# Threshold arithmetic of a sparse-attention kernel: three steps per four heads moved from GpSimd to VectorE

## What is computed

```python
scores = einsum('bhqd,bhkd->bhqk', Q, K) / sqrt(16)       # 16 heads, 512 keys
thresh = top_k(scores, 31)[0][..., -1:]
scores = where(scores < thresh, -inf, scores)
context = einsum('bhqk,bhkd->bhqd', softmax(scores), V)
```

## Time and profile before

| what | value |
|---|---|
| median of three runs | 4140.59 us (4138.47 to 4140.77) |
| the profiled execution | 4140.48 us |
| its span, first to last instruction | 4138.7 us |
| granted TensorE clock, mean of the span | 0.977 |
| TensorE / VectorE / GpSimd / ScalarE busy | 94% / 93% / 86% / 85% of the span |
| the chain that ended last, by engine | PE 42%, POOL 31%, DVE 18%, ACT 4% |

### The profile page before, as it was taken

The page is one execution under the profiler, slowest core; times in us unless marked ns, Lnnn a source line. Parts: engine busy times, 40 slices in busy tenths (PEclk is TensorE's granted clock), DMA queues, the critical chain, the costliest instruction groups (busy, mean ns, idle before and its releaser), DMA issues.

```text
span 4138.7 us, 97302 instructions
## 1 busy us (share of the span) xinstructions
PE 3891.9 (94%) x31052; PEld 3201.5 (77%) x31052; DVE 3858.8 (93%) x15296; ACT 3530.2 (85%) x7749; POOL 3556.2 (86%) x4554
## 2 busy tenths in 40 slices
PE   6878999999999999999999999999999999998777
PEld 5656788888888888888888888888888888876566
DVE  3399999999999999999999999999999999999982
ACT  3389989989999998999999899999989999998872
POOL 1578999999999999999999999999999999987650
PEclk8889999999999999999999999999999999999988
DMA  3211221212222122222212222222222222121112
GB/s 108 54 34 35 56 63 53 63 56 62 54 58 63 52 63 55 62 55 58 63 52 63 55 60 58 57 61 54 61 56 60 57 58 60 54 50 28 31 29 57
DMA packets 243955, 230.71 MB, mean 56 GB/s; under 512 B 27123, under 2 KB 176628, under 8 KB 243316
## 3 DMA queue, kind: packets, MB, share of 16 engines
q1 hardware_dynamic: 243444, 224.49, 20.7%
HBM read 214.98 MB, written 9.44 MB: 54 GB/s over the span
## 4 chain that ended last, share of the span: by engine, by line
PE 42%; POOL 31%; DVE 18%; ACT 4%; issue 3%; DMA 1%; SPq 0%; POOLq 0%; ACTq 0%; DVEq 0%
PE pQ L592 15%; POOL HS L353 10%; POOL HL L965 5%; POOL HL L964 5%; PE pST L610 4%; PE pST L577 3%; POOL RB L364 3%; PE pFb L553 3%; PE pO L631 3%; DVE HL L915 2%; DVE HL L909 2%; DVE HL L905 2%; DVE HL L901 2%; DVE M L917 2%; DVE M L913 2%
## 5 line engine op out<-in xcount | busy, mean ns | idle before, releaser
L592 PE MATMUL pQ<-wf_sb,HS 128*128 128x192 f32 x8192 | 1474.9, 335 | 87.1 <-POOL HS L353 66.0
L592 PEld LDWEIGHTS pQ<-wf_sb,HS 128*128 128x128 f32 x8192 | 1361.6, 194 | 164.2 <-issue 107.2
L797 ACT ACTIVATE S<-S,edge 128x512 f32<-128x512 f32 x1024 | 743.3, 726 | 7.7 <-POOL edge L952 7.6
L803 ACT ACTIVATE S<-S,lift 128x512 f32<-128x512 f32 x1024 | 747.2, 730 | 1.9
L964 POOL TENSOR_TENSOR HL<-S,HL 128x512 f32<-128x512 f32 x512 | 657.3, 1284 | 12.8 <-ACT S L780 12.8
L965 POOL TENSOR_TENSOR HL<-S,HL 128x512 f32<-128x512 f32 x512 | 657.4, 1284 | 0.0
L610 PE MATMUL pST<-ident,S 128*128 128x128 f32 x4096 | 513.6, 276 | 68.6 <-ACT S L803 41.4
L353 POOL TENSOR_TENSOR HS<-hT_a,RB 128x1024 f32<-128x1024 f32 x244 | 577.8, 2368 | 0.3 <-issue 0.3
L353 POOL TENSOR_TENSOR HS<-hT_b,RB 128x1024 f32<-128x1024 f32 x240 | 568.1, 2367 | 4.1 <-PE pQ L592 2.7
L610 PEld LDWEIGHTS pST<-ident,S 128*128 128x128 f32 x4096 | 460.1, 142 | 107.1 <-ACT S L803 61.1
L780 ACT COPY S<-pST 128x1024 f32<-128x1024 f32 x512 | 494.6, 1025 | 23.1 <-PE pST L577 22.2
(11 more groups left out here) (255 smaller groups left out, 7228.4 us busy)
## 6 DMA issues: line engine op xcount, KB each, us to landing
RB<-rows_b SPq DMA_DIRECT2D x384, 256.0 KB, 3.4
RB<-rows_a SPq DMA_DIRECT2D x384, 256.0 KB, 3.4
x_b<-in_x SPq DMA_DIRECT2D x64, 128.0 KB, 2.1
out_y<-y SPq DMA_DIRECT2D x64, 128.0 KB, 3.1
wf_sb<-in_wf SPq DMA_DIRECT2D x4, 768.0 KB, 7.1
rows_b<-rwT SPq DMA_DIRECT2D x64, 8.0 KB, 1.3
wof_sb<-in_wof SPq DMA_DIRECT2D x1, 1024.0 KB, 7.4
rows_a<-rwT SPq DMA_DIRECT2D x64, 8.0 KB, 1.3
```

The lines of the kernel that those rows point to most:

```text
L592: mm = nc.tensor.matmul(pQ[:, 0:QKV], HS[:, m % 2, e, i, :], wf_sb[:, i, at:at + QKV], start=k + e + i == 0, stop=(k, e, i) == (3, 3, 1))
L797: nc.scalar.activation(S[:, r, :], S[:, r, :], ACT.Prelu, bias=edge[:, r:r + 1], scale=-2.0, alpha=1.0 / STEEP).then_inc(s_cut, 1)
L803: nc.scalar.activation(S[:, r, :], S[:, r, :], ACT.Exp, bias=lift[:, r:r + 1], scale=-0.5 * STEEP).then_inc(s_gap, 1)
```

## The change

Queries, their bias and so all scores are formed at half size (`keep` and `qbias` take an extra factor of 0.5), and the exponential's scale is doubled from -0.5 `STEEP` to -`STEEP`. With halved scores h the sum of ranks 31 and 32 is already the middle of the two full-size scores, so `half` and its step are not needed, and `lift` is the sum of four neighbouring columns of `M8`: h31, h32 and two columns in which the negated maximum is written. `M8` grows from 32 to 34 columns. VectorE computes all of it with reductions of one operand; GpSimd's three steps go. Two slot tables decide where: `EDGE` (new, 10.5 + 4n) holds the first two reductions, `LIFT` (12.25 + 4n, as before, now on VectorE) the third.

```diff
+AT["EDGE"] = series(10.5, 4, QUADS)
 AT["LIFT"] = series(12.25, 4, QUADS)
...
-        M8 = sb("M8", P, RING, RANKS)
+        M8 = sb("M8", P, RING, RANKS + 2)
...
-                    nc.scalar.activation(S[:, r, :], S[:, r, :], ACT.Exp, bias=lift[:, r:r + 1], scale=-0.5 * STEEP
+                    nc.scalar.activation(S[:, r, :], S[:, r, :], ACT.Exp, bias=lift[:, r:r + 1], scale=-STEEP
...
-                nc.vector.memset(keep[32 * h:32 * h + HD, 0:1], HD ** -0.5)
+                nc.vector.memset(keep[32 * h:32 * h + HD, 0:1], 0.5 * HD ** -0.5)
...
-                    nc.vector.tensor_scalar(qbias[:], bias[:, :, :, 0], HD ** -0.5, None, ALU.mult).then_inc(s_kb, 1)
+                    nc.vector.tensor_scalar(qbias[:], bias[:, :, :, 0], 0.5 * HD ** -0.5, None, ALU.mult).then_inc(s_kb, 1)
...
+                if (n := WHEN["EDGE"].get(s)) is not None:
+                    rows = M8[:, 4 * n % RING:4 * n % RING + HG, :]
+                    wait(dve, s_tk, searched(4 * n + 3))
+                    nc.vector.tensor_reduce(edge[:, 4 * n % RING:4 * n % RING + HG], rows[:, :, TH:TH + 2],
+                                            mybir.AxisListType.X, ALU.add).then_inc(s_edge, 1)
+                    nc.vector.tensor_reduce(rows[:, :, RANKS:RANKS + 2], rows[:, :, 0:1].unsqueeze(3).broadcast_to([P, HG, 2, 1]),
+                                            mybir.AxisListType.X, ALU.max, negate=True).then_inc(s_top, 1)
+                if (n := WHEN["LIFT"].get(s)) is not None:
+                    r = 4 * n % RING
+                    wait(dve, s_top, n + 1)
+                    nc.vector.tensor_reduce(lift[:, r:r + 4], M8[:, r:r + 4, TH:TH + 4], mybir.AxisListType.X, ALU.add
+                                            ).then_inc(s_lift, 1)
...
-                if (n := WHEN["LIFT"].get(s)) is not None:
-                    r = 4 * n % RING
-                    wait(pool, s_tk, searched(4 * n + 3))
-                    nc.gpsimd.tensor_tensor(edge[:, r:r + 4], M8[:, r:r + 4, TH], M8[:, r:r + 4, TH + 1], ALU.add
-                                            ).then_inc(s_edge, 1)
-                    pool.wait_ge(s_edge, n + 1)
-                    nc.gpsimd.tensor_scalar(half[:, r:r + 4], edge[:, r:r + 4], 0.5, None, ALU.mult).then_inc(s_mid, 1)
-                    pool.wait_ge(s_mid, n + 1)
-                    nc.gpsimd.tensor_tensor(lift[:, r:r + 4], half[:, r:r + 4], M8[:, r:r + 4, 0], ALU.subtract
-                                            ).then_inc(s_lift, 1)
```

More of the change, by code:

```diff
@@ L194, in build @@
         HL = sb("HL", P, RINGH, HIL + HALVES)
-        M8 = sb("M8", P, RING, RANKS)
+        M8 = sb("M8", P, RING, RANKS + 2)
         edge = sb("edge", P, RING)
-        half = sb("half", P, RING)
         lift = sb("lift", P, RING)
@@ L254, in build @@
         s_kb, s_bop, s_bo, s_half = sem("s_kb"), sem("s_bop"), sem("s_bo"), sem("s_half")
-        s_kd, s_hi, s_lo, s_dif, s_rd, s_edge, s_mid = (
-            sem(n) for n in ("s_kd", "s_hi", "s_lo", "s_dif", "s_rd", "s_edge", "s_mid"))
+        s_kd, s_hi, s_lo, s_dif, s_rd, s_edge, s_top = (
+            sem(n) for n in ("s_kd", "s_hi", "s_lo", "s_dif", "s_rd", "s_edge", "s_top"))
         s_sc, s_ev, s_tk, s_cut, s_lift, s_gap, s_pt, s_pe, s_pv, s_oc, s_ot, s_o, s_vm = (
@@ L851, in _ @@
             nc.vector.memset(keep[:, 0:1], 0.0)
-            nc.vector.memset(keep[:, 1:2], HD ** -0.5)
+            nc.vector.memset(keep[:, 1:2], 0.5 * HD ** -0.5)
             nc.vector.memset(V[:], 0.0).then_inc(s_ini, 1)
```

## The result

| | median us | range, runs | ratio to before (95% interval) |
|---|---|---|---|
| before | 4140.6 | 4138.5 to 4141.6, 5 | |
| changed | 4159.4 | 4159.2 to 4163.4, 5 | 1.0048 (1.0037 to 1.0059) |

The change makes the kernel 18.8 us slower, 0.48%. The span went from 4138.7 to 4157.4 us. Forecast was 4172.

What follows compares the result with a forecast made beforehand. VectorE, with the least time to spare, was taken as the bound. 61.7 + 16.3 - 1.8 - 45.6 + 3.0 - 2.5 = +31.1 us on 4140.6 gave 4172 us, range 4155 to 4203.

Steps and rivals of the forecast that it cites:

- About no change: Rival: VectorE's reductions at the low end, 0.212 us per quad, dependency on L917 hidden; +5, 4146 us; chance 0.09.
- three reductions and the lost overlap behind L917: On VectorE: three reductions per quad, +61.7 us; lost overlap and small gap at 139 places, +16.3 us.
- VectorE's waits: VectorE's idle time, nearly all in front of L879 waiting for ScalarE's L727, would go: -45.6 us.
- waits that stay: On VectorE: allowance because L879 and L907 still stand behind other engines, +3.0 us.
- start: Pipeline fill before 272 us: six quads are searched where VectorE idles, so their new steps cost nothing, -1.8 us.
- end: End of the search: GpSimd's wait at L952, with L353 behind it, goes; -2.5 us, between 0 and -3.
- the 10 ns between L871 and L873: VectorE's reductions: difference perhaps the price of one more number written; steps taken as 72, 82 and 87 ns.
- The gap behind L917: On VectorE: a reduction directly behind L917 loses 0.083 us of overlap and idles 0.034 us, 0.117 us each.
- the bound that I had set for being wrong: Sign: the prediction is wrong if the period, forecast near 243 us, falls below 241.8 us.
- The third step comes late: Rival: ScalarE's L803 waits for L928 behind a pair search; 20 us of VectorE's waits stay, 4189 us; chance 0.21.
- No overlap: Rival: each reduction holds VectorE for its whole length, 490 ns instead of 241, +64 us, 4236 us; chance 0.04.
- VectorE has room and the kernel gets faster: Rival: GpSimd's relief shortens the middle if VectorE's new steps cost under 0.18 us per quad; 4130 us; chance 0.04.

Runs made afterwards that it cites:

- the earlier lift: The changed kernel with negated maximum, edge and lift, in this order, all behind the second pair search: 4155.8 us (1.0040).
- The second copies: The changed kernel with each of the three reductions issued twice, the second time into a tile that nothing reads: 4215.8 us (1.0178).
- the other place: The changed kernel with all three reductions inside the first pair search of the next quad: 4137.8 us (0.9999).

## Why the prediction was right, and where its sum was off

**The bound.** VectorE's order of work, with its 45.6 us of waits as the only thing to set against new work: right. The chain is 92% VectorE, no wait is left, and forecasts from this order alone came within 11 us in six kernels (4142.0 for 4143, 4161.0 for 4159, 4215.8 for 4211, 4137.8 for 4142, 4155.8 for 4150, 4099.8 for 4110). They fail only where lift comes later still (4333.7 for 4159, 4181.9 for 4160), and there VectorE waits again. The forecast of 4172 lies 12.6 us above the result, 31.1 us of change against 18.8. The number alone would not decide, since the rival "About no change" (4146) is as near, 13.4 us away. What decides is the price per quad, below, which is neither that rival's 0.212 us nor the forecast's 0.305.

The terms, one by one, for the 250 quads searched behind the sixth where a term concerns these:

| term | predicted us | measured us |
|---|---|---|
| three reductions and the lost overlap behind L917 | 76.2 | some 70 |
| VectorE's waits | -45.6 | some -50 |
| waits that stay | +3.0 | 0 |
| start (already without the six quads) | 0 | +3.1 |
| end | -2.5 | -4.2 |
| sum | 31.1 | 18.7 |

*The reductions* were mis-sized. The groups in the trace of the changed kernel:

```profile
L921 DVE TENSOR_REDUCE edge<-M 128x4 f32<-128x8 f32 x256 | 40.1, 157 | 4.7
L923 DVE TENSOR_REDUCE M<-M 128x8 f32<-128x8 f32 x256 | 39.0, 152 | 0.0
L928 DVE TENSOR_REDUCE lift<-M 128x4 f32<-128x16 f32 x256 | 36.4, 142 | 0.0
```

and the steps in order of time, a lift and an edge behind L917:

```profile
2033.83 0.43 DVE L917 MAX8 M<-HL 128x8 f32<-128x272 f32 x1
2034.17 0.15 DVE L928 TENSOR_REDUCE lift<-M 128x4 f32<-128x16 f32 x1
2034.24 0.75 DVE L899 MAX8 M<-HL 128x8 f32<-128x256 f32 x2
...
2040.73 0.78 DVE L917 MAX8 M<-HL 128x8 f32<-128x272 f32 x2
2041.54 0.16 DVE L921 TENSOR_REDUCE edge<-M 128x4 f32<-128x8 f32 x1
2041.62 0.15 DVE L923 TENSOR_REDUCE M<-M 128x8 f32<-128x8 f32 x1
2041.69 0.74 DVE L899 MAX8 M<-HL 128x8 f32<-128x256 f32 x2
```

L928 starts at 2034.17 and L899 at 2034.24; L921 at 2041.54, L923 at 2041.62, L899 at 2041.69. From start to start they take some 78, 68 and 68 ns, 0.214 us per quad, where I had taken 72, 82 and 87, 0.241. The step that failed is the one on the 10 ns between L871 and L873, which I shared out over the numbers written: L923 writes eight numbers and takes as long as L928 with four. So the number written is not the price. Where a step stands does change its length: edge is 157 ns long here and 143 inside the next search. *The gap behind L917* is as predicted: L917 ends at 2041.51 and L921 starts 0.03 later, an idle of 4.7 us in all (137 x 34 ns; the two L928 that I had counted with them show none), and the kernel with the two steps elsewhere is 17.4 us faster, with 16.3 predicted. 0.214 and the 0.063 that I had for the gap make 0.277 per quad, 69 us for 250. The search of the kernel with a single step on GpSimd, where VectorE has the order of before and no wait, is 71.3 us shorter than that of the changed kernel (3700.8 and 3772.1), which says nearly the same.

*The waits* gave back more than their idle time. In the search 19.8 us came; with 69 us of new order, some 50 must have gone, so the table's -50 is a remainder. The kernel with a single step on GpSimd shows 51.5. The 45.6 left out the overlap that is lost at each of the 47 waits, 3.9 us in all.

*Waits that stay*: none did. My reason for their going was wrong in part: I had TensorE come earlier because GpSimd is lighter. With GpSimd as loaded as before they are gone too; that VectorE is later by its own 0.28 us per quad is enough, 16 x 0.277 = 4.4 us per period against 4.2.

*Start and end*: the late lift costs 3.1 us where the pipeline fills (I had put nothing there, since VectorE idles). At the end I had -2.5, because GpSimd's L353 no longer stands behind the wait for a search, and -4.2 came. But the runs do not show that this wait is the cause. Where GpSimd waits for no search, the last part takes 110.0 to 114.4 us (110.4 in the changed kernel, 114.4 with lift early, and 117.8 with the latest lift), and where it does 108.6 to 114.6. So the size of this term fits by luck at least in part, and its cause stays open.

*The signs.* VectorE's busy time is 3920.7 us for the 3930 forecast. GpSimd's is 3409.8 for 3393: part of the steps' time had overlapped other steps. The reductions' lengths are 142 to 157 ns for 145 to 190. The period is 241.8 us for 243, just at the bound that I had set for being wrong. L803's waits were to come in the last stretch, 4 us at most; they reach 6.6 us, and 47.9 of the 125 us lie between 580 and 3600 us.

**The rivals.** *The third step comes late*: it does, ScalarE waits 125 us for it, and in the middle this costs nothing, as the earlier lift showed. But it is the right thing to fear: 2.9 us later it costs 22 us, 7.2 us later 174, for the most part through TensorE. *No overlap*: out. The second copies cost 71 ns each at a length of 151 to 159. The rule of the Trainium skill (VectorE: DVE Perf Modes, the section on the DRAIN), by which the next step waits for an empty pipeline, does not describe these steps. The same section excepts a step that is not held and refers to the one on two instructions with no wait between them; the trace agrees with this exception, L923 starts 0.08 us after L921, which is 0.16 long. *VectorE has room and the kernel gets faster*: it would have, had the steps been fewer. The relief of GpSimd is worth having, -34 us with one step less and -58 with two, but the three reductions cost 0.277 us per quad against the limit of 0.18 that I gave. *About no change* is what the same three reductions give at the other place (0.9999).

## What to carry to other kernels

Work that is moved off a loaded engine is paid for by the engine that takes it: compare its price with the idle time that this engine has left, not with what the giving engine saves. Here 0.8 us per quad went from GpSimd and 0.28 came to VectorE, and the kernel became slower, because VectorE had 0.18 (0.21 with the overlap that its waits cost). Price a small step by the distance from its start to its successor's, and don't put it right behind the step it reads: two places four steps on were worth 17 us. And before moving work, ask whether it must be done: dropping one of the three small steps and leaving the others where they were gave 34 us, and unchaining them 42, both with halved scores and only a part of the row maximum taken out of the exponent.

## What was not expected of the hardware

- The step behind a small reduction on VectorE starts some 70 ns after it: 68 in most places, whether it reads 8 or 16 numbers and writes 4 or 8, 78 behind a gap, and 59 or 76 at some places inside a search. The profile gives it a length of 142 to 164 ns.
- Directly behind the step that it reads, a reduction starts 118 ns later than another step would: 34 ns of idle time and some 84 of lost overlap.
- A wait costs VectorE more than its idle time: 51.5 us came back for 45.6 us of waits. The 84 ns of overlap lost at each make up 3.9 of the 5.9 us between them; the other 2.0 us lie at steps that did not wait.
- A copy that is late by 1.2 us on ScalarE reaches VectorE some 35 us later, because TensorE works without a break between the two (the runs with a late lift).
- The length that the profile gives a small step depends on its neighbours: lift was 142 ns long in the changed kernel and 164 ns behind another reduction.
